# Score masks as two half-height products behind the value chunks, and VectorE's rsqrt state in the second output bank

## The reference

```
x = x + 0.5 * F(layernorm(x))
x = x + scan(layernorm(x))      # h = x W_in + b_in; state = sigmoid(a) state + b h; y W_out + b_out
x = x + 0.5 * F(layernorm(x))

F, for each of 6 layers:
  q, k, v = shift(x) @ Wqkv            # 16 heads of 64
  q, k = l2norm(.) * scale, then rotary
  out = softmax(8 q k^T, masked) v     # windows of 32: a window sees itself and the one before,
                                       # masked where j > i or j < i - 32, or before the start
  x = out @ Wo + x
  xn = layernorm(shift(x)) * g + b
  x = (xn @ W1a + b1a) * gelu(xn @ W1g + b1g) @ W2 + b2 + x
```

## Time and profile before

| | us |
|---|---|
| median of 3 runs | 3271.0 (3269.25 to 3271.45) |
| the profiled execution, its own time | 3267.9 |
| its span in the trace | 3266.1 |
| TensorE busy | 3181.2 (97%) |
| VectorE busy | 2751.1 (84%) |
| ScalarE busy | 2456.6 (75%) |
| GpSimd busy | 2226.2 (68%) |

### The profile page before, as it was taken

One profiled execution on the slowest core, in us unless ns is written; L12 is line 12 of the kernel. 1 busy time (PEld: TensorE's weight loads), 2 busy tenths in 40 slices (PEclk: granted clock), 3 DMA queues, 4 the chain that ended last, 5 costly groups with the idle time before them and its releaser, 6 DMA issues. The chain is left out here.

```text
span 3266.1 us, 154583 instructions
## 1 busy us (share of the span) xinstructions
PE 3181.2 (97%) x63464; PEld 2373.5 (73%) x63464; DVE 2751.1 (84%) x6950; ACT 2456.6 (75%) x3760; POOL 2226.2 (68%) x1453
## 2 busy tenths in 40 slices
PE   7999999999999999999999999999999999999998
PEld 3777777777777777777777777777777777777776
DVE  6888888888888888889999888888888888888885
ACT  3777777777777777777777777777777777777775
POOL 5666666666666666667887766666666666666663
PEclk8999999999999999999999999999999999999999
DMA  4111111111111111111111111111111111111111
GB/s 130 49 50 48 48 49 43 49 47 50 47 51 47 50 48 50 47 49 51 44 51 43 50 52 48 50 47 51 47 50 48 47 50 43 48 47 50 51 54 39
DMA packets 198869, 164.28 MB, mean 50 GB/s; under 512 B 139667, under 2 KB 172567, under 8 KB 198551
## 3 DMA queue, kind: packets, MB, share of 16 engines
q1 hardware_dynamic: 193943, 157.05, 17.7%
q10 hardware_dynamic: 4608, 3.34, 0.3%
HBM read 33.38 MB, written 1.05 MB: 11 GB/s over the span
## 5 line engine op out<-in xcount | busy, mean ns | idle before, releaser
L1097 POOL TENSOR_TENSOR rot<-rot,swp 128x1024 f32<-128x1024 f32 x384 | 906.8, 2362 | 140.7 <-DVE rot L891 140.7
L510 PE MATMUL proj<-wq,xsT 128*128 (+1 forms) x1536 | 772.3, 624 | 40.8 <-issue 29.8
L703 ACT ACTIVATE sq<-proj 128x512 f32<-128x512 f32 x768 | 437.7, 596 | 448.8 <-PE proj L510 436.7
L1106 POOL TENSOR_TENSOR rot<-rot,rn 128x1024 f32<-128x1024 f32 x384 | 724.2, 1907 | 0.0
L1087 POOL TENSOR_TENSOR rt<-rt,half 128x1 f32<-128x1 f32 x192 | 105.4, 549 | 704.5 <-DVE rt L961 704.5
L885 DVE TENSOR_TENSOR swp<-proj,tab 128x512 f32<-128x512 f32 x768 | 523.1, 681 | 10.0 <-ACT sq L703 9.3
L1015 DVE SCALAR_TENSOR_TENSOR hT<-proj,cols,fg 114x128 f32<-114x128 f32 (+1 forms) x576 | 166.7, 344 | 422.0 <-ACT fg L769 418.1
L891 DVE TENSOR_TENSOR rot<-proj,tab 128x512 f32<-128x512 f32 x768 | 517.4, 674 | 0.6 <-PE tps L521 0.6
L521 PEld LDWEIGHTS tps<-idf,rot 128*128 128x128 f32 x3072 | 360.0, 141 | 205.0 <-issue 202.1
L1091 POOL TENSOR_TENSOR prob<-prob,rr 128x1024 f32<-128x1024 f32 x192 | 365.4, 1903 | 175.3 <-DVE rr L973 175.3
L510 PEld LDWEIGHTS proj<-wq,xsT 128*128 128x128 f32 x1536 | 259.6, 190 | 272.0 <-issue 215.5
(11 more groups left out here) (99 smaller groups left out, 5833.5 us busy)
## 6 DMA issues: line engine op xcount, KB each, us to landing
vb<-va SPq DMA_DIRECT2D x192, 384.0 KB, 3.5
vb<-va SPq DMA_DIRECT2D x192, 128.0 KB, 3.4
wq<-in_L_ffn_Wqkv SPq DMA_DIRECT2D x95, 192.0 KB, 2.6
xs<-Z SPq DMA_DIRECT2D x384, 32.0 KB, 2.2
xs<-Z SPq DMA_DIRECT2D x384, 28.0 KB, 2.0
xs<-Z SPq DMA_DIRECT2D x384, 3.8 KB, 2.0
xs<-Z SPq DMA_DIRECT2D x384, 0.2 KB, 1.7
wo<-in_L_ffn_Wo SPq DMA_DIRECT2D x94, 64.0 KB, 2.2
```

What stands on the lines that cost most here:

```text
L510: mm(proj[:, c % 2, :], xsT[:, k.parity(L_QKV), :], wq2[:, bass.ds(w + c * 512, 512)], start=True, stop=True).then_inc(p_qkv[c], 1)
L703: fn(sq[:, c * 512:(c + 1) * 512], proj[:, c % 2, :], ACT.Square).then_inc(a_sq[c], 1)
L1097: g_.tensor_tensor(r, r, swp[:, g * INNER:(g + 1) * INNER], ALU.add).then_inc(g_add[g], 1)
L1106: g_.tensor_tensor(r, r, rn[:, g * HEADS:(g + 1) * HEADS].unsqueeze(2) .to_broadcast([P, HEADS, DH]), ALU.mult).then_inc(g_nm[g], 1)
```

## The change

The two masks are no longer whole products at the head of the scores. Each has 64 rows: the identity is replaced by a "spread" matrix in which row r feeds both columns with the same window row, so that 64 rows of mask give 128 rows of scores. The first uses rows 0 to 63 and writes bank 0 of `sps`, the second rows 64 to 127 and bank 1. They stand behind the value chunks and ahead of the xs transposition, and wait in addition for `a_xnT`, since the xn transposition shares bank 1. So that they need not wait for the rsqrt state, that state moves to bank 1 of `ops`. VectorE's first sum of squares now waits for `a_oT` in place of `v_sub`, and TensorE waits for `v_rs` of the step before ahead of the q transpositions and `attend`. W2 (and the two products of `middle`) leave bank 1 of `ops` for bank 0 and stand in front of Wo; who reads them waits for `p_wo`, as Wo writes the same bank. The cast of the identity to bf16 at the start becomes a transfer of the spread matrix by way of `oT` and a cast in step 1.

```diff
             def idle(n):
-                    mm(ops[:, 1, 0:3 * P], ...
+                    mm(ops[:, 0, 0:3 * P], ...

+            def masks(k):
+                first = k.off("first", L_S, lambda u: ((POS - 1 - u % POS) // (POS - 1)) * 512)
+                for ty, at in ((0, bass.ds(first, 512)), (1, slice(0, 512))):
+                    rows = slice(ty * DH, (ty + 1) * DH)
+                    mm(sps[:, ty, :], idb[rows, :], mask[rows, at], start=True, stop=False, skip_group_check=True)
+
             def scores(k):
-                first = k.off("first", L_S, lambda u: ((POS - 1 - u % POS) // (POS - 1)) * 512)
                 par = k.parity(L_S)
-                for ty in range(2):
-                    m = mask[:, bass.ds(first, 512)] if ty == 0 else mask[:, 0:512]
-                    mm(sps[:, ty, :], idb[:, :], m, start=True, stop=False, skip_group_check=True)
...
                 if k.on(L_AV):
...
                     k.wait(v_z, L_F2 + 1, base=TILES)
+                    k.wait(v_rs, L_QKV + 1, per=RS_STEPS)
...
                     transpose_rot(1, p_kT)
+                if k.on(L_F2):
...
+                    k.wait(v_h, L_F2)
+                    k.wait(a_oT, L_AV)
...
+                    at = k.layer(L_F2, 3 * P)
+                    for c in range(3):
+                        last = mm(ops[:, 0, P:2 * P], hT[0:FC, c, :], w2[0:FC, bass.ds(at + c * P, P)],
+                                  start=(c == 0), stop=(c == 2))
+                    last.then_inc(p_f2, 1)
                 if k.on(L_WO):
...
                     tr(sps[:, 1, 0:P], xn[:, :], idf[:, :]).then_inc(p_xnT, 1)
-                if k.on(L_F2):
...
-                        last = mm(ops[:, 1, 3 * P:4 * P], hT[0:FC, c, :], w2[0:FC, bass.ds(at + c * P, P)],
-                                  start=(c == 0), stop=(c == 2))
-                    last.then_inc(p_f2, 1)
...
                     values(k, 0)
+                if k.on(L_S):
+                    k.wait(v_sub, L_S + 1)
+                    k.wait(a_qT, L_S)
+                    k.wait(a_kT, L_S)
+                    if k.parity(L_S) == 0:
+                        k.wait_even(a_car, L_S)
+                    k.wait(a_xnT, L_F)
...
+                    masks(k)
                 if k.on(L_X):
...
                 if k.on(L_S):
 
-                    k.wait(v_sub, L_S + 1)
-                    k.wait(v_rs, L_QKV, per=RS_STEPS)
-                    k.wait(a_qT, L_S)
-                    k.wait(a_kT, L_S)
-                    if k.parity(L_S) == 0:
-                        k.wait_even(a_car, L_S)
...
                     scores(k)
...
-            xsq, rsq, usq = [sps[:, 0, 2 * HEADS * n:2 * HEADS * (n + 1)] for n in range(3)]
+            xsq, rsq, usq = [ops[:, 1, 2 * HEADS * n:2 * HEADS * (n + 1)] for n in range(3)]
...
                     k.wait(a_sq[0], L_QKV)
-                    k.wait(v_sub, L_S + 1)
+                    k.wait(a_oT, L_AV)
...
                     k.wait(p_f2, L_F2)
+                    k.wait(p_wo, L_WO)
                     k.wait(d_xs2, L_F2 - 1, per=64)
...
-                    v.tensor_tensor(zs, zs, ops[:, 1, 3 * P:4 * P], ALU.add).then_inc(v_z, 1)
+                    v.tensor_tensor(zs, zs, ops[:, 0, P:2 * P], ALU.add).then_inc(v_z, 1)
```

More of the change, by code:

```diff
@@ L618, in body @@
                     transpose_rot(1, p_kT)
+                if k.on(L_F2):
+                    if k.reg is None and k.s == L_F2:
+                        pe.wait_ge(d_late, 16 * len(late_consts))
+                    k.wait(v_h, L_F2)
+                    k.wait(a_oT, L_AV)
+                    if k.mid(M_IN) is not None:
+                        k.wait_mid(m_xT, M_IN)
+                        mm(ops[:, 0, 2 * P:3 * P], winT[:, :], mx_t[:, :], start=True, stop=True, skip_group_check=True)
+                    if k.mid(M_OUT) is not None:
+                        k.wait_mid(m_y, M_OUT)
+                        mm(ops[:, 0, 3 * P:4 * P], ys[:, k.mid(M_OUT) % 2, :], woutT[:, :], start=True, stop=True,
+                           skip_group_check=True)
+                    at = k.layer(L_F2, 3 * P)
[3 more added lines that the diff above has]
+                    last.then_inc(p_f2, 1)
                 if k.on(L_WO):
@@ L661, in body @@
                     values(k, 0)
+                if k.on(L_S):
[5 more added lines that the diff above has]
+                    k.wait(a_xnT, L_F)
+                    if k.reg is None and k.s == L_S:
+                        pe.wait_ge(s_idb, 1)
+                        pe.wait_ge(s_mask, 1)
+                    masks(k)
                 if k.on(L_X):
@@ L788, in between @@
                 elif s == 1:
-                    act.wait_ge(d_mask, 16)
+                    act.wait_ge(d_mask, 32)
+                    cp(idb[:, :], oT[:, 0, :]).then_inc(s_idb, 1)
                     cp(mask[:, :], prob[:, :, :, :].rearrange("p a b c -> p (a b c)")).then_inc(s_mask, 1)
@@ L901, in middle @@
                 if t is not None:
-                    k.wait(p_f2, L_F2)
+                    k.wait(p_wo, L_WO)
                     k.wait_mid(m_bo, M_OUT)
-                    v.tensor_tensor(xb[:, t, :], xb[:, t, :], ops[:, 1, P:2 * P], ALU.add).then_inc(m_x2, 1)
+                    v.tensor_tensor(xb[:, t, :], xb[:, t, :], ops[:, 0, 3 * P:4 * P], ALU.add).then_inc(m_x2, 1)
                 t = k.mid(M_IN)
                 if t is not None:
-                    k.wait(p_f2, L_F2)
-                    v.tensor_scalar(mbh[:, :], ops[:, 1, 0:P], cols[:, RAW_C:RAW_C + 1], cols[:, RAW_C + 2:RAW_C + 3],
+                    k.wait(p_wo, L_WO)
+                    v.tensor_scalar(mbh[:, :], ops[:, 0, 2 * P:3 * P], cols[:, RAW_C:RAW_C + 1], cols[:, RAW_C + 2:RAW_C + 3],
                                     ALU.add, ALU.mult).then_inc(m_bh, 1)
@@ L1214, in _constants @@
     row = np.arange(P)
-    i, g = (row % WIN)[:, None], (row // (2 * WIN))[:, None]
+    i, g, low = (row % WIN)[:, None], (row % (2 * WIN) // WIN)[:, None], (row < 2 * WIN)[:, None]
     j = (np.arange(512) % (2 * WIN))[None, :]
     usual = ((j < WIN) & (j >= i)) | ((j >= WIN) & (j - WIN <= i))
-    first = np.where(g == 0, usual & (j >= WIN), usual)
+    first = np.where((g == 0) & low, usual & (j >= WIN), usual)
     mask = np.concatenate([np.where(m, 0.0, NEG) for m in (usual, first)], 1).astype(f)
-    return {"rope": rope, "mask": mask, "ident": np.eye(P, dtype=f)}
+    spread = ((i == i.T) & (g == (row // (2 * WIN))[None, :])).astype(f)
+    return {"rope": rope, "mask": mask, "ident": np.eye(P, dtype=f), "spread": spread}
 def kernel(**inputs):
```

10 lines of the change are left out of this document (3 added, 7 removed).

## The result

| | before | after |
|---|---|---|
| median of the runs | 3271.0 (3269.25 to 3271.9) | 3283.28 (3281.97 to 3284.62) |
| the profiled execution, its span | 3267.9, 3266.1 | 3283.2, 3281.4 |

The ratio is 1.0043, with a 95% interval of 1.0033 to 1.0054: the change makes the kernel 12.3 us slower. The forecast was 39 us slower (3310, range 3260 to 3328). The sign and the new wait are right, the size is a third of what was said. "Before" and "after" mean the two kernels of this case throughout.

What follows compares the result with a forecast made beforehand. The prediction took a cycle through TensorE, ScalarE's oT copy and VectorE to bind at 16.77 us a step against 16.52; 165 steps x 0.25 = 41 us took 3267.9 to 3309, median 3310, range 3260 to 3328.

Steps and rivals of the forecast that it cites:

- entry and exit: On TensorE around the two half-height masks: switching into the tiled form costs 0.10 us and out of it 0.12.
- the rival of no change: Masks on TensorE cost no drain or bare load and overlap: M 0.22, 0.06 a step faster, 3261 us; chance 0.20.
- the serial one: Masks run one behind the other with all switches: M 0.80, 0.45 a step, 3345 us; chance 0.10 together with W2 felt.
- The unheld VectorE chain: Chain over ScalarE and VectorE through one step, without its wait for the square of chunk 0: 16.46 us.
- M: Price on TensorE of the two half-height masks between value products and xs transposition: 0.59 us, bounds 0.22 to 0.80.
- bare bf16 load: Weight load ahead of the masks on TensorE, no longer hidden: 0.05 us, an estimate of half the fp32 load.
- bare fp32 load behind: Weight load on TensorE after the masks, before the next fp32 products, not hidden: 0.10 us.
- the a_oT cycle: xs transposition, TensorE to square 0, ScalarE to oT, first sum, last rot product, next xs transposition: 16.77 us a step.
- TensorE's leg: TensorE from xs transposition to square of chunk 0: 5.82 us, minus 0.58 removed, plus 0.59 added, unchanged within 0.01.
- rival "partly": One end cheap, loads hidden, or serial without drain: M 0.35 to 0.50, 0 to 0.15 a step, 3272 to 3296; chance 0.15.
- 165 steps with the full price: 192 steps less 19 in the outer layer and 8 at start and refills, each 0.25 us slower: 41 us.
- the main case: The masks pay all form changes but overlap, M 0.50 to 0.65: 3295 to 3321 us; chance 0.55.

Runs made afterwards that it cites:

- sums in the score bank: Changed kernel with VectorE's two sums of squares written to bank 0 of sps and the a_oT wait moved to the later maximum: 3267.4 us, ratio 0.9990.
- the two last runs: Changed kernel with the long-met waits repeated before the scores in steps written out singly, 3292.3 us; changed kernel with only the mask products moved back there, 3292.1 us.

## Why the prediction was right or wrong

**Right.** The sign, and for the reason given: the wait alone costs 63 us, and TensorE's part of the change doesn't make up for it. The first sum of squares follows the end of the oT copy by 0.09; oT copy to sum is 1.105, forecast 1.02 + 0.09 = 1.11. Square 0 to oT is unchanged. The masks run side by side, 0.003 apart. They don't hide the change of form: entry and exit are paid, so the rival of no change falls, and so does the serial one. The hidden products have no gap, scores start 0.20 behind the last of them. Once moved, W2 is hidden as long as the a_oT cycle binds (W2 moved back: same time), and it is felt without it (sums in the score bank, 0.11 a step; forecast up to 0.14). The unheld VectorE chain was put at 16.46 and ran at 16.45. The start, put at within 1 us, took none. Not quite right: VectorE is held for 0.17 ahead of the sum, not 0.25, since its own list now comes 0.07 later against the oT copy.

**Wrong, first: the size of M.** The step that failed is the sum of the masks' price.

| term | forecast | measured |
|---|---|---|
| entry into the 64-row form | 0.10 | 0.096 |
| bare bf16 load | 0.05 | 0 |
| stream, both | 0.22 | 0.216 |
| exit | 0.12 | 0.105 |
| bare fp32 load behind | 0.10 | 0.055 |
| M | 0.59 | 0.47 |

The measured terms come from three medians: last value product to masks 0.525, of which 0.429 is the product; masks to T 0.321, of which 0.216 is the stream; T to hidden 0.165 where it was 0.110. Their names, entry, exit and load, are the forecast's. The load ahead of the masks doesn't show in addition to the entry, and the load behind costs half of the 0.10 that I had read from groups of four products. So TensorE's leg is 0.14 shorter than before, not 0.01 longer. Of the 0.15 between the two 0.12 is M; 0.03 are small gains elsewhere in the leg. It goes the other way that a sum which had to wait takes 0.06 longer, which I had not in the cycle. The forecast's 16.77 becomes 16.77 - 0.12 - 0.03 + 0.06 = 16.68, and the edges after add up to 16.69. Before they add up to 16.53, and the median step is 16.54, where I had 16.52. That makes 0.14 to 0.16 a step and not 0.25. The forecast's rival "partly" (M of 0.35 to 0.50, 3272 to 3296) was the case that came.

**Wrong, second: 165 steps with the full price and the rest with none.** In the 146 steps outside the outer layer and the start, 0.25 each would be 36.5 us; they took 20.1, which is 0.14 each. In the outer layer's 34 steps I had 19 at nothing and 15 at 0.25, 3.8 us; they took -5.0. The start and the end took -0.1 and 0.2. Together that is 15.3, the difference of the spans; the medians of the runs lie 12.3 apart.

**Not priced at all: the stalls in the score products.** The earlier trace rows show them: 16.4 us of "issue" at L553. I read the row for its 225 ns and passed over its idle column. Moving five waits and the masks away from the scores took 12 us of it, and 10 us of the maximum's waiting. In the outer layer the maximum waited 4.8 us less, about what that stretch gained. With masks and waits back the change costs 28 us instead of 12. That the waits' place is the cause in the steps written out one by one is shown by the two last runs; at the entries of the loops the products' place counts as well. Why a wait that is met makes TensorE run dry some products later, and only in code it comes to for the first time, no run here shows: that the instructions arrive late and the sequencer loses its lead over them at the waits would fit, but is argued only.

So the main case had the right cycle with a wrong price in it, and the rest was made by terms that went both ways and that the forecast didn't have.

## What to carry to other kernels

Price a moved product by the form of what stands around it: the same two half-height masks saved 0.09 a step where they shared the scores' change of form, cost 0.04 more than whole ones where they had it alone, and made no difference where another engine set the step. When state changes banks, look for what reads the new bank late in the step. Here one wait cost 0.30 a step, twice what TensorE won. Moving only the first writes (the sums) away from it turned +12 us into -3, and W2 back in its old place, which made no difference as long as that wait stood, turned -3 into -21. A move that is hidden behind one wait is to be tried again once that wait is gone. And read the idle column of long runs of small products: semaphore waits moved away from in front of them were worth some 5 us in the outer layer here, though they never held anything up.

## What the runs showed of the hardware

- Going from full products into 64 rows by 128 columns costs TensorE 0.096 us and back 0.105, plus 0.055 until the next fp32 products run. That is about what the changes to the 64 x 32 and 64 x 64 forms cost in the earlier trace rows. From the half-height masks straight to the scores' form it is 0.104. Two 64-row products of 512 columns in different row halves and banks start 0.003 us apart.
- VectorE products of 32 columns with both inputs in SBUF took 2256 ns where they met a GpSimd product, and ended 0.05 us behind it; while GpSimd was idle they took 174, and 178 with one input in PSUM.
- A VectorE sum over 1024 columns that had to wait for its semaphore takes 1.23 us in place of 1.17. In the one run with a further semaphore wait in front of it, it started 0.11 us later.
- Inside 128 score products TensorE can stand still for over 1 us (1.19 in the step shown) with nothing to wait for that the profile shows, in steps whose code is new to it. Waits in front of these products that are long met go with 7.1 to 13.9 us of such idle time in the outer layer, the same waits further ahead with 2.2 to 4.5.
